# Twenty products that nobody reads, placed in TensorE's order in the last part of the self-attention

## The reference

```python
x = x + cross_attention(layernorm(x), ctx)      # one head of 512, keys and values from ctx
x = x + self_attention(layernorm(x))            # 16 heads of 32, low-rank q and kv (128), causal, @ W_o.T
h = layernorm(x)
x = x + routed_experts(h) + shared_expert(h)    # top 4 of 16 experts (256 wide), relu squared; shared 1024 wide
```

## Time and profile before

| | us |
|---|---|
| median of 3 runs | 372.35 |
| lowest, highest run | 371.6, 373.34 |
| profiled execution, span from first to last instruction | 375.5 |
| TensorE busy in it | 342.0 (91%) |
| VectorE busy | 243.5 (65%) |
| ScalarE busy | 189.5 (50%) |
| GpSimd busy | 82.8 (22%) |
| mean granted TensorE clock | 0.968 of full speed |

### The profile page before, as it was taken

How to read it: one execution, slowest core, us unless ns; L and a number is a source line. 1 busy time by engine, 2 the same in 40 slices (tenths; PEclk the granted TensorE clock), 3 DMA queues, 4 the chain that set the end, 5 groups by cost and what they waited for, 6 DMA issues and landing times.

```text
span 375.5 us, 6906 instructions
## 1 busy us (share of the span) xinstructions
PE 342.0 (91%) x2500; PEld 238.9 (64%) x2500; DVE 243.5 (65%) x478; ACT 189.5 (50%) x425; POOL 82.8 (22%) x103
## 2 busy tenths in 40 slices
PE   1998979999999998987979789999999989999996
PEld 1976757677777756766868667988644444444344
DVE  3665767566479647837666675992434676778677
ACT  2456455543576475455455561522134586777620
POOL 4500000000001211312223314004346635432100
PEclk9999889999999999999867899999999999999999
DMA  6892499885332228047000047579934444331472
GB/s 194 314 389 96 174 376 415 318 293 197 114 141 92 85 86 307 7 170 301 0 31 0 31 168 254 209 267 410 398 114 155 164 139 136 120 113 58 180 299 112
DMA packets 17185, 69.70 MB, mean 186 GB/s; under 512 B 2816, under 2 KB 3328, under 8 KB 14592
## 3 DMA queue, kind: packets, MB, share of 16 engines
q1 hardware_dynamic: 13632, 57.72, 41.5%
q0 software_dynamic: 3520, 11.54, 8.8%
HBM read 61.91 MB, written 7.34 MB: 184 GB/s over the span
## 4 chain that ended last, share of the span: by engine, by line
PE 70%; DVE 15%; ACT 6%; issue 4%; another core or an unknown queue 1%; POOL 1%; DMA 1%; DVEq 0%; SPq 0%; ACTq 0%
PE bank L1723 9%; PE bank L1336 9%; PE bank L1691 9%; PE bank L1338 8%; PE bank L1337 8%; PE bank L1564 8%; ACT hw L790 2%; PE bank L1660 2%; PE bank L1463 2%; PE bank L1734 2%; DVE cT L1103 2%; PE bank L1702 2%; PE bank L1489 2%; PE bank L1534 1%; PE bank L1473 1%
## 5 line engine op out<-in xcount | busy, mean ns | idle before, releaser
L1564 PE MATMUL bank<-ring,wT 128*128 128x384 f32 x128 | 43.9, 486 | 0.0
L1691 PE MATMUL bank<-WX,xsT 128*32 128x256 f32 (+1 forms) x256 | 38.0, 380 | 2.5 <-DVE xsT L1246 1.3
L1723 PE MATMUL bank<-WX,hsT 128*32 128x512 f32 (+1 forms) x128 | 38.2, 598 | 0.0
L1103 DVE TENSOR_TENSOR cT<-ring_T,cT 128x512 fp32r<-128x512 f32 x48 | 30.5, 686 | 5.8 <-ACT cT L673 5.8
L1691 PEld LDWEIGHTS bank<-WX,xsT 128*32 128x32 f32 x256 | 17.7, 110 | 23.8 <-issue 13.8
L1564 PEld LDWEIGHTS bank<-ring,wT 128*128 128x128 f32 x128 | 23.7, 190 | 13.4
L673 ACT CAST cT<-ring_T 128x512 fp32r<-128x512 f32 x48 | 26.8, 618 | 10.1 <-PE bank L1338 10.1
L569 POOL TENSOR_TENSOR rstd<-var,mhalf 128x1 f32<-128x1 f32 x12 | 7.4, 614 | 111.0 <-DVE var L904 111.0
L1691 PE MATMUL bank<-up_copy,xsT 128*32 128x256 f32 x384 | 30.9, 380 | 0.0
L1723 PE MATMUL bank<-down_copy,hsT 128*32 128x512 f32 x192 | 30.7, 598 | 0.0
L1268 DVE COPY down_copy<-WX 128x1024 f32 x32 | 20.8, 690 | 14.6 <-PE bank L1723 14.6
(11 more groups left out here) (282 smaller groups left out, 866.3 us busy)
## 6 DMA issues: line engine op xcount, KB each, us to landing
WX<-in_experts SPq DMA_DIRECT2D x16, 1024.0 KB, 6.9
ring_T<-in_ctxT SPq DMA_DIRECT2D x16, 768.0 KB, 7.2
ring<-in_ctx SPq DMA_DIRECT2D x16, 768.0 KB, 4.4
WX<-y_rows SPq DMA_DIRECT2D x4, 1024.0 KB, 8.1
raw<-in_experts SPq DMA_DIRECT2D x3, 1024.0 KB, 4.9
res<-in_x SPq DMA_DIRECT2D x4, 256.0 KB, 5.3
raw<-in_wqT SPq DMA_DIRECT2D x4, 256.0 KB, 4.8
raw<-in_woT SPq DMA_DIRECT2D x1, 1024.0 KB, 11.0
```

The lines of the kernel that those rows point to most:

```text
L1103: V_.tensor_tensor(cT[:, g % 2, 1, t, :], ring_T[:, g % RING_T, t, :], f32(cT[:, g % 2, 0, t, :]), ALU.subtract).then_inc(cTlo_ok, 1)
L1564: last = mm(bank[B_O][:, 0:TD], wT[:, g % 2, k * P:(k + 1) * P], ring[:, g % RING, k, :], start=(c == 0 and k == 0), stop=(c == NCH - 1 an ...
L1691: last = mm(bank[B_H[g % 2]][q * SLOT:(q + 1) * SLOT, 0:IC * P], xsT[:, g % 2, c * P + q * SLOT:c * P + (q + 1) * SLOT], w, start=c == 0, ...
L1723: last = mm(bank[B_Y[g % 2]][q * SLOT:(q + 1) * SLOT, :], hsT[:, g % 2, m * P + q * SLOT:m * P + (q + 1) * SLOT], w, start=m == 0, stop=m ...
```

## The change

A table `SPARE` names three steps, and at the head of each of these TensorE's order has 6, 8 and 6 products of a 128 x 128 tile of the normalised rows' high part (`xT_h`, batch row 0) by 512 columns of `W_o`'s high part. Each is a group of its own (start and stop), all write PSUM bank 4, none waits for a semaphore or signals one, and nothing reads what they write. The other engines' orders are untouched.

```diff
+        SPARE = {23: 6, 25: 8, 28: 6}
...
+            def spare_products(n):
+
+                for _ in range(n):
+                    mm(bank[B_O][:], xT_h[:, 0, tok(0)], wo_w[:, 0, 0:D], start=True, stop=True)
+
             for step in range(1, STEPS):
+                spare_products(SPARE.get(step, 0))
                 if (u := unit_at(step, 0)) is not None and u % 2 == 0:
                     pair_scores(u)
```

## The result

The change made the kernel a little slower. The median of 20 runs is 373.11 us (372.05 to 374.57) against 371.89 us (370.19 to 373.56) in 20 runs of the kernel before; the ratio is 1.0037 with a 95% interval of 1.0023 to 1.0051, so 0.9 to 1.9 us. Forecast were 370.0 us and a range of 368.3 to 373.0.

What follows compares the result with a forecast made beforehand. TensorE, busy 342.0 of 375.5 us, was taken to bound the kernel, with three slow-clock stretches partly on the path. Terms 1.1 + 1.6 - 0.3 = 2.4 us gave 373.1 us profiled, 370.0 us median, range 368.3 to 373.0.

Steps and rivals of the forecast that it cites:

- The first term: Slow stretch 177.75 to 181.10 us, after step 23: full clock starts the scores of unit 12 1.1 us earlier.
- The second: Slow stretch 191.40 to 201.60 us: full clock gains 1.6 us up to the scores of unit 14, bounds 0.4 and 1.8.
- The third term: Slow stretch 211.85 to 215.20 us, step 28: between +0.6 and -0.8 us, taken as -0.3.
- Rival A: Slow stretches move rather than go: 0 to 1 us gained, 371.8 us; chance 0.20.
- Rival B: Added products in steps 23, 25 and 28 run slow and end late: 376.0 us or about 374.2; chance 0.12.
- C: Gain given back after the attention, in experts' loads or unrelated waits: 0 to 1 us gained, 371.9 us; chance 0.08.
- D: All three slow stretches are on the path: 8.5 us gained, 363.9 us as a median; chance 0.03.

Runs made afterwards that it cites:

- step 25 alone: Kernel before with only the 8 added products of step 25: 372.32 us, ratio 1.0016.
- the narrow ones: Kernel before with 6, 6 and 8 added products in steps 23, 25 and 26, each 16 columns wide and not 512: 372.63 us, ratio 1.0030.
- all five groups: Kernel before with 6, 6, 8, 6 and 4 added products in steps 23, 25, 26, 28 and 30: 368.85 us, ratio 0.9927.
- Group three alone: Kernel before with only the 6 added products of step 28: 373.36 us, ratio 1.0047.
- change and step 30: The changed kernel with 4 more products at the head of step 30: 370.98 us, ratio 0.9957 to the kernel before.
- second profile of before: The kernel before, unchanged, profiled again: 372.14 us, ratio 1.0002; profiled span 370.4 us.

## Why the prediction was wrong

*The first term held.* Forecast: the scores of unit 12 start 1.1 us earlier after unit 10's; measured 1.14 us, and they lasted 1.16 us. In timed runs the group is worth less, 0.7 us (0.9981), with an interval that takes in no gain at all, since the clock doesn't fall in step 23 in every execution: in the profile with step 25 alone, where step 23 has no products, it did not, nor in that of the narrow ones.

*The second was sized too high.* Forecast 1.6 us from unit 12 to 14, measured 1.0. The slow stretch in step 26 that I named came (193.1 to 196.5), and I had priced it within 0.2 us. It cost 0.6: with all five groups, where it is missing, the same way takes 9.33 us, so the full 1.6 us were there to be had. The transposes of unit 11 took 1.12 us in place of 0.66, and ScalarE copies them (from 194.72 us, where the kernel with all five groups has 194.17) before it turns to the exponentials of unit 13; the forecast had only the products behind them slow. GpSimd's scaling of unit 11, too, took 1.93 us in place of 1.04, but it did so in the kernel with all five groups as well, so that is not what was lost. In step 25 the eight products were priced against an idle time of 1.99 us taken from a profile with a slow stretch in step 23; with that gone the cover is smaller, they end 0.4 us behind ScalarE's exponentials (188.08 and 187.64), and the next scores start 0.2 us later than behind six (2.92 and 2.71 us after the start of the product before).

*The third term is the step that failed.* I wrote "Between +0.6 and -0.8 I take -0.3". Group three alone costs 1.7 us (1.0047 [1.0023, 1.0070]), and in the changed profile the part is 1.0 us longer. The mechanism is the one priced there, a slow stretch moved from step 28 to steps 30 and 31, and its price for a stretch was right: from the weights of unit 15 to the product of step 31 it takes 6.16 us with it and 4.76 without (change and step 30), 1.4 us. The gain to set against it was 0.4 (5.15 to 4.76), not 0.6, for GpSimd's end of unit 15 did not move (215.36 and 215.29): 0.4 - 1.4 = -1.0. Wrong was to take the middle between two outcomes when the own text had found that the gain was capped by GpSimd and the loss wasn't.

*A second term that failed was put at nothing.* "From there the chain is TensorE and VectorE without slack", so what was won at step 31 would be won at the end. At step 31, 2.4 us were forecast and 1.2 measured; behind it, in the changed profile and in that of step 28 alone, stands another slow stretch (251.1 and 254.2) that begins among the last of the routing's 32 narrow products or 0.4 us behind them and costs 1.34 us (151.29 against 149.95). So the span is 370.7 us against 370.4. None of the other twelve profiles has it, and with step 30 filled each level of the change's runs has two slow stretches fewer. By this it comes with the one in steps 30 and 31, and chance is an unlikely reading; why one brings the other is open. It is also what the prediction named as a sign of its being wrong: the scores of unit 14 start early and the last instruction does not.

*The baseline was one unlucky execution.* The forecast scaled a gain from a profile with seven slow stretches to a median whose runs have four to eight. Its own bounds, added up, gave 0.3 to 4.0 us gained, so no choice within them would have given a loss. Rival A had the right mechanism (the stretches move rather than go) but not its sign: it took 0.5 to 1 us off a gain of 1.1, and the two that stand in new places cost 2.7 us together. Rival B played no part in the changed kernel, whose added products ran at full clock. C foretold a gain lost after the attention; that happened, but by TensorE's clock and not by loads or waits. D played none: the slow 17 us were worth at most the 3.3 us that the kernel with all five groups gains over the second profile of before (370.4 to 367.1), not 8.5.

## What to carry to other kernels

A slow stretch of TensorE's clock is worth only what the chain waits for in it: first ask of each whether another engine covers it, and leave the covered ones alone, or fill every thin stretch behind them as well. Here, six products in step 28 alone lost 1.7 us, and with four more in step 30 they lost nothing; a thin stretch left open behind a filled one is where the loss went. And before a gain is read off one profile, look how the runs divide by granted clock, and take the baseline from more than one.

## What the runs showed of the hardware

- The clock fell to 1.2 GHz without a long pause. In the profile of before the longest waits just ahead of a slow stretch were 1.99 us and 2.08 us (at 51.39 us); in the changed one it fell at 193.1 us, within a wait of 2.58 us, and at 251.1 us with no wait above 0.4 us in the 8 us ahead, behind 3.1 us of products of 40 columns. In the kernel with all five groups it stayed up over a wait of 1.22 us in step 28.
- Slow stretches lasted 3.4 us, or two or three times that, in every profile, and what one cost went by its place: 0.6 us in step 26, 1.4 in steps 30 and 31, 1.34 behind the routing, 1.8 with the one at 51.5 us, and 0.4 in step 28, where ScalarE and GpSimd cover it.
- GpSimd's product of 128 x 512 with a broadcast took 1.04 us in some places and 1.93 us in others: the long ones began just behind a VectorE subtraction of two SBUF tiles. In the changed profile, GpSimd and VectorE:

```profile
191.59 1.93 POOL L588 TENSOR_TENSOR hw<-hw,hrd 128x512 f32<-128x512 f32 x1 [4.27 <-DVE hrd L938]
```

```profile
191.42 1.20 DVE L895 TENSOR_TENSOR u_w<-raw,u_w 128x1024 fp32r<-128x1024 f32 x1
```

It goes the other way too: in the first profile of before GpSimd began at 194.86 us and took its 1.04, and VectorE's subtraction of the same kind, begun at 195.09, took 1.88 us. The page SBUF — State Buffer of the Trainium skill (SBUF: two separate sides, under "Reading the diagram") says that a VectorE instruction with two SBUF inputs and a GpSimd instruction that reads SBUF share a pair of ports, which goes to whichever starts first for its whole instruction. The trace agrees: GpSimd took 0.9 us more behind a 1.20 us instruction begun 0.17 us earlier, and VectorE 0.7 us more behind GpSimd's.
